# Two attention blocks and an MLP on one core: u's halves moved ahead of three scalings and of the inputs' normalisation, the mask's subtraction moved from VectorE to ScalarE

## The chip, the core and the metric

The kernel runs on one core of one Trainium2 chip. The metric is the device time of one execution in microseconds. Five engines work side by side, each through its own list of instructions in the order in which it was written: TensorE (PE, with its weight loads shown apart as PEld), VectorE (DVE), ScalarE (ACT), GpSimd (POOL), and SyncE (SP), which here issues every DMA. They meet only at semaphores: an instruction waits until a counter has reached a value, and all that is written behind it on its engine waits with it.

## The reference, cut to what matters

For 64 batches of x and ctx, each 128 x 512 in float32:

```python
Mn = Wn @ inorm(x) + bn;  Mm = Wm @ inorm(ctx) + bm        # inorm: normalised over the last axis
A = softmax(Mn.T @ Mm)                                      # 512 x 512
x1 = Wo @ ((Wl @ ctx + bl) @ A.T) + bo + x                  # first attention block
q, k, v = ln(x1) @ q_w + q_b, ctx @ k_w + k_b, ctx @ v_w + v_b     # 16 heads of 32
attn = softmax(where(mask, q @ k.T * scale, lowest))        # mask: one value for each key
hidden = (attn @ v) @ cproj_w + cproj_b + x1                # second attention block
out = hidden + gelu(ln(hidden) @ fc_w + fc_b) @ proj_w + proj_b
```

## The kernel before, in words

Two passes follow each other. `attention_pass` makes `hidden` for all 64 batches, `mlp_pass` makes the output. The change touches the first alone.

Every float32 operand of a large product is split into two halves: `hi`, the value rounded to the format of TensorE's fast float32 (an activation on ScalarE), and `lo`, the rest (a subtraction on VectorE or GpSimd). A product is three matmuls (L966, L967, L968: hi x lo, lo x hi, hi x hi).

The pass is a software pipeline over "slots". In slot s each engine works on several batches at once, each in another stage of its way: b0 = s is in the first block's scores, a1 = s-1 in the transposition of its A, b1 = s-2 in u and the output of the first block (x1), b2 = s-3 in V and the transposition of the normalised x1, b3 and b4 in the second block's scores and softmax, b5 = s-6 in the output projection, and `ahead` = s+1 in the normalisation of its inputs. There are 70 slots; those in the middle are a loop whose body holds four. Even and odd slots differ in one thing: a pair of batches shares the projection to the queries (L688 on ScalarE) in the one kind and to the keys (L682) in the other. Below they are called slots of queries and slots of keys. Nothing but the order in the code sets the order on an engine.

What stands around the change in one slot:

- TensorE: scores of the second block (four matmuls with the mask, L1053, then 64 small ones, L1058), V, the transposition of x1n (L997), Mn and Mm, the first half of queries or keys, the first block's scores, attn @ v (L1099), U = ctxT x at in twelve matmuls, the second half of queries or keys, OUT0 = Wo Wl x u (three matmuls that read `u_hi` and `u_lo`, in the profile `bank<-m_lo,small_hi` and its two neighbours, since u lies in the tile m), and the output projection (reads `qc`).
- ScalarE: exponentials, the hi half of outT (L732), four scalings of A by the reciprocal of its row sums (L738), the hi half of u (L742), the hi halves of the transposed A in four pieces (L710, two and two, with the bias of queries or keys between), the hi halves of the two normalised inputs (L751), the hi half of ctxT (L758).
- VectorE: two transpositions of A's blocks (L842), the lo half of outT (L805), the normalisation of the two inputs of `ahead` (L913), two more transpositions (L842), the lo half of u (L805 again), the transposition of ctx (L926), x1 (L931) and its statistics (L934), the mask less one (L939), hid (L952), maxima of the second scores (L829), x1n, which is x1 normalised (L851).
- GpSimd: at_lo in four pieces (L599), the lo halves of the inputs (L614), the deviation of x1 (L620), x1 plus a bias (L626, tile `stage`), the lo half of ctxT (L629), then the other two pieces of at_lo. VectorE's x1n waits for L626, since it overwrites x1 which L626 reads.
- SyncE: all loads in one queue. The load of the next inputs (L438, L439) waits for the normalisation L913, since it overwrites x_ctx; behind it stand p_blocks, a_turn (A written to DRAM), blocks, hidden, and the next slot's a_blocks (A read back, which waits for a_turn to have landed and for at_lo).

The mask of the second block is loaded as bytes; `mask_less_1` is mask - 1 in bfloat16, and TensorE adds it, times the largest value, to the scores.

Of the kernel before, what the change touches and what calls it, by code (L numbers as in the profile page):

```python
# [18 lines left out]
ALU = mybir.AluOpType  # L19
ACT = mybir.ActivationFunctionType  # L20
AX_X = mybir.AxisListType.X

P = 128
# [164 lines left out]
def attention_pass(nc, x, ctx, mask, w, hidden, mlp):  # L188
# [3 lines left out]
    DC = D // P  # L192
# [4 lines left out]
    with ExitStack() as stack:  # L197
        def sb(name, shape, dt=F32):
            return stack.enter_context(nc.sbuf_tensor(name, shape, dt))
# [68 lines left out]
        rsum0 = sb("rsum0", [P, DC])  # L268
# [3 lines left out]
        x1_rstd = sb("x1_rstd", [P, 1])  # L272
        mask_u8 = sb("mask_u8", [P, 2, P], U8)
        mask_less_1 = sb("mask_less_1", [P, P], BF16)
        negmax1 = sb("negmax1", [P, 4, 4])
        sum1 = sb("sum1", [P, 4, 4])
        rsum1 = sb("rsum1", [P, 4, 4])
# [150 lines left out]
        def _(sp):  # L428
# [78 lines left out]
            def slot(s):  # L507
                if (s + -1).exists():
                    read_a(s + -1)
                e = s + -2  # L510
                if e.exists():
                    if e.has_before(1):
                        after(x1_set, (e + -1).nth(1, 1))
                    else:
                        sp.wait_ge(wow_copied, 2)
                    sp.dma_start(x_res, x[e.number]).then_inc(x_res_loaded, 16)
                e = s + -4
                if e.exists():
                    u = e.parity
                    if e.has_before(2):  # L520
                        after(mask_set, (e + -2).nth(1, 1))
                    else:
                        sp.wait_ge(consts_set, 3)
                    sp.dma_start(mask_u8[0:P:32, u, :],
                                 mask[e.number].partition_broadcast(4)).then_inc(mask_loaded[u], 16)
                if s.first():
                    load_weight(C_W)
                if (s + -5).exists():
                    write_probs(s + -5, 0)
                    write_probs(s + -5, 1)  # L530
                e = s + 2
                if e.exists() and e.has_before(2):
                    load(e)
                if (s + -5).exists():
                    read_probs(s + -5)
                if s.exists():
                    write_a(s, 0)
                    write_a(s, 1)
                e = s
                if e.exists() and e.has_before(1):  # L540
                    load_blocks(e)
                e = s + -6
                if e.exists():
                    after(hid_set, e.nth(1, 1))
                    sp.dma_start(hidden[e.number], hid[:]).then_inc(hid_stored[e.parity], 16)
# [23 lines left out]
        def _(pool):  # L569
# [1 line left out]
            pool.wait_ge(ident_zero, 1)  # L571
            pool.affine_select(out=ident[:], in_=ident[:], compare_op=ALU.not_equal, fill=1.0, base=0,
                               pattern=[[-1, P]], channel_multiplier=1).then_inc(ident_set, 1)
            pool.wait_ge(consts_set, 3)

            def lower_halves(i):

# [67 lines left out]
        def _(act):  # L645
# [18 lines left out]
            def slot(s):  # L664
# [52 lines left out]
                def exp0(t):  # L717
                    if b0.exists():
                        if t == 0 and a1.exists():
                            act.wait_ge(a_written, a1.nth(32, 32))  # L720
                        act.wait_ge(max0_set, b0.nth(4, t + 1))
                        act.activation(A[:, :, t, :], by_chunk(S0_BANK[t]), ACT.Exp,  # L722
                                       bias=negmax0[:, t:t + 1],
                                       accum_out=sum0[:, t:t + 1]).then_inc(exp0_done, 1)

                exp0(0)
                exp0(1)
                exp0(2)
# [5 lines left out]
                    first_weights(1)  # L734
                if b0.exists():
                    act.wait_ge(rsum0_set, b0.nth(1, 1))
                    for t in range(DC):
                        act.activation(A[:, :, t, :], A[:, :, t, :], ACT.Identity,  # L738
                                       scale=rsum0[:, t:t + 1]).then_inc(a_scaled, 1)
                if b1.exists():  # L740
                    act.wait_ge(u_done, b1.nth(1, 1))
                    act.activation(u_hi, bank[U_BANK][:], ACT.Copy).then_inc(u_hi_set, 1)  # L742
                upper_at(0)
                upper_at(1)
                qk_bias(1)
# [2 lines left out]
                if ahead.exists():  # L748
                    for i in range(2):
                        act.wait_ge(normed_set, ahead.nth(2, i + 1))  # L750
                        act.activation(normed_hi[:, i, :], normed[:, i, :], ACT.Copy).then_inc(normed_hi_set, 1)  # L751
                if a1.exists():
                    act.wait_ge(ctxT_turned, a1.nth(1, 1))
                    if b2.exists():
                        act.wait_ge(v_done, b2.nth(1, 1))
                        if s.parity == 1:
                            act.wait_ge(k_done, b2.pair_nth(2, 2))
                    act.activation(pair_half(ctxT_hi, a1), ctx_chunks, ACT.Copy).then_inc(ctxT_hi_set, 1)  # L758
# [4 lines left out]
        def _(dve):  # L763
            dve.memset(masked_bf[:], MASKED).then_inc(consts_set, 1)
            dve.memset(neghalf[:], -0.5).then_inc(consts_set, 1)
            dve.memset(mask_u8[:], 0).then_inc(consts_set, 1)
            dve.wait_ge(consts_set, 3)

            def prepare_small():
                dve.wait_ge(small_in, 16 * 8)  # L770
# [40 lines left out]
            def slot(s):  # L811
# [91 lines left out]
                if b5.exists():  # L903
                    dve.wait_ge(outT_hi_set, b5.nth(1, 1))
                    lower(outT_lo, bank[PV_BANK][:], outT_hi, outT_lo_set)
                if ahead.exists():

                    dve.wait_ge(in_rstd_ready, ahead.nth(1, 1))
                    if b0.exists():
                        dve.wait_ge(m_done, b0.nth(2, 2))  # L910
                        dve.wait_ge(normed_lo_set, b0.nth(2, 2))
                    for i, src in enumerate((x_in, ctx_in)):
                        dve.tensor_scalar(normed[:, i, :], src, in_mv[:, i, 0:1],  # L913
                                          in_rstd[:, i:i + 1], ALU.subtract, ALU.mult).then_inc(normed_set, 1)
                turn_a(2)
                turn_a(3)
                if b1.exists():
                    dve.wait_ge(u_hi_set, b1.nth(1, 1))
                    lower(u_lo, bank[U_BANK][:], u_hi, u_lo_set)
                if b5.exists() and not b4.exists():  # L920
                    first_group()
                if a1.exists():
# [5 lines left out]
                if b1.exists():  # L928
# [3 lines left out]
                                             in1=x_res, op0=ALU.add, op1=ALU.add).then_inc(x1_set, 1)  # L932
                    dve.wait_ge(x1_set, b1.nth(1, 1))
                    dve.bn_stats(x1_stats[:], x1[:]).then_inc(x1_stat, 1)  # L934
                if b3.exists():
                    dve.wait_ge(mask_loaded[b3.parity], b3.dma())
                    if b3.has_before(1):
                        dve.wait_ge(s1_done, (b3 + -1).nth(1, 1))
                    dve.tensor_scalar(mask_less_1[:], mask_u8[:, b3.parity, :], -1.0, None,  # L939
                                      ALU.add).then_inc(mask_set, 1)  # L940
                if b1.exists():
                    dve.wait_ge(x1_stat, b1.nth(1, 1))
                    dve.sem_inc(stats_seen, 1)
# [517 lines left out]
```

## Time and profile before

| | us |
|---|---|
| median of 3 runs | 3034.93 |
| the 3 runs | 3034.93, 3034.04, 3037.51 |
| the profiled execution | 3036.39 |
| its span in the trace | 3034.5 |
| PE busy | 2864.3 (94%) |
| DVE busy | 1910.4 (63%) |
| ACT busy | 1469.5 (48%) |
| POOL busy | 1119.3 (37%) |

The attention pass takes the first 1665 us of the span, roughly; the MLP pass takes the rest and keeps TensorE busy nearly without a gap. Times in a trace are counted from the start of the span. Rows of a timeline give start, duration, engine, line, operation, the written and the read tiles, and how many like instructions were merged; in square brackets stands how long the engine had been idle before it and what ended that. The chain that ended last runs through the MLP pass alone and says nothing of the attention pass.

### The profile page before, as it was taken

The numbers are of one execution on the slowest core, as the hardware profiler recorded it, in microseconds if no ns is written. First come the engines' busy times: TensorE is split into PE (matmuls) and PEld (weight loads), VectorE is DVE, ScalarE is ACT, GpSimd is POOL, SyncE is SP. The second block draws the span as 40 slices with busy tenths as digits, with TensorE's granted clock in tenths as the row PEclk, the third lists the DMA queues.
The fourth block names the chain that finished last, engine by engine and source line by source line (L and its number), as shares of the span: only waits on it lengthen the run. The fifth ranks groups of instructions, "written<-read, shape, count | busy, mean of one in ns | idle before, by whom it ended". The sixth has DMA issues, their size and how long they took to land. (4 is left out here: it accounts for less than half of the span.)

```text
span 3034.5 us, 54536 instructions
## 1 busy us (share of the span) xinstructions
PE 2864.3 (94%) x17527; PEld 2369.3 (78%) x17527; DVE 1910.4 (63%) x3705; ACT 1469.5 (48%) x4210; POOL 1119.3 (37%) x998
## 2 busy tenths in 40 slices
PE   5899999999999999999977999999999999999999
PEld 3777777777777777777765888888888888888887
DVE  5799899999989899999855433333333333333332
ACT  5788778887878877888743211111111111111111
POOL 5566666666666666666632000000000000000000
PEclk7999999999999999999997999999999999999999
DMA  6588888888888888888863210101111111011110
GB/s 184 164 237 230 231 238 229 239 229 235 232 227 237 228 235 236 232 235 232 226 175 129 69 40 17 41 28 41 41 41 41 29 27 39 30 41 41 41 28 14
DMA packets 440889, 416.65 MB, mean 137 GB/s; under 512 B 155200, under 2 KB 319552, under 8 KB 440768
## 3 DMA queue, kind: packets, MB, share of 16 engines
q1 hardware_dynamic: 440768, 415.40, 49.4%
q14 instruction: 89, 0.73, 0.1%
q8 instruction: 32, 0.52, 0.1%
HBM read 231.79 MB, written 167.77 MB: 132 GB/s over the span
## 5 line engine op out<-in xcount | busy, mean ns | idle before, releaser
L1306 ACT ACTIVATE gl<-pre,fc_bias 128x512 f32<-128x512 f32 x256 | 176.6, 690 | 1119.4 <-PE pre L1391 1119.4
L1345 DVE CAST hT_hi<-gl 128x512 fp32r<-128x512 f32 x256 | 109.3, 427 | 840.2 <-ACT gl L1306 840.2
L673 ACT ACTIVATE rows<-bank,negmax 128x128 f32<-128x128 f32 x1024 | 364.2, 394 | 209.2 <-DVE negmax L829 198.9
L599 POOL TENSOR_TENSOR at_lo<-a_blocks,at_hi 128x512 fp32r<-128x512 f32 x256 | 335.4, 1330 | 190.1 <-ACT at_hi L710 190.1
L590 POOL TENSOR_TENSOR rows<-rows,rsum 128x512 f32<-128x512 f32 x256 | 266.0, 1040 | 271.4 <-DVE rsum L825 271.4
L177 POOL TENSOR_TENSOR rstd<-ve,neghalf 128x4 f32<-128x4 f32 x16 | 16.3, 1018 | 870.9 <-DVE ve L171 870.9
L1390 PE MATMUL pre<-yT_hi,rest_lo 128*128 128x512 f32 x768 | 298.9, 389 | 0.0
L1389 PE MATMUL acc<-rest_lo,hT_hi 128*128 128x512 f32 x768 | 298.9, 389 | 0.0
L1391 PE MATMUL acc<-rest_hi,hT_hi 128*128 128x512 f32 x768 | 298.9, 389 | 0.0
L1391 PE MATMUL pre<-yT_hi,rest_hi 128*128 128x512 f32 x768 | 298.8, 389 | 0.0
L1389 PE MATMUL pre<-yT_lo,rest_hi 128*128 128x512 f32 x768 | 298.8, 389 | 0.0
L1390 PE MATMUL acc<-rest_hi,hT_lo 128*128 128x512 f32 x768 | 298.8, 389 | 0.0
L673 ACT ACTIVATION_READ_ACCUMULATOR rows<-bank,negmax 128x1 f32 x1024 | 239.9, 234 | 0.0
L1266 POOL TENSOR_TENSOR rows<-rows,proj_bias 128x512 f32<-128x512 f32 x64 | 82.9, 1298 | 326.4 <-DVE y L183 321.2
L829 DVE TENSOR_REDUCE negmax<-bank 128x4 f32<-128x512 f32 x256 | 169.0, 682 | 36.7 <-PE bank L1058 36.7
L722 ACT ACTIVATE rows<-bank,negmax 128x512 f32<-128x512 f32 x256 | 178.0, 782 | 10.5 <-DVE negmax L835 10.5
L1347 DVE TENSOR_TENSOR hT_lo<-gl,hT_hi 128x512 fp32r<-128x512 f32 x256 | 177.3, 692 | 8.8
L738 ACT ACTIVATE rows<-rows,rsum 128x512 f32<-128x512 f32 x256 | 164.3, 714 | 26.8 <-DVE rsum L900 26.8
L842 DVE STREAM_TRANSPOSE a_blocks<-a_blocks 128x512 f32<-128x512 f32 x256 | 166.2, 687 | 8.3 <-DMA a_blocks<-a_turn 7.6
L614 POOL TENSOR_TENSOR normed_lo<-x_ctx,normed_hi 128x512 fp32r<-128x512 f32 x128 | 162.2, 1289 | 23.5 <-ACT normed_hi L751 23.4
L835 DVE TENSOR_REDUCE negmax<-bank 128x1 f32<-128x512 f32 x256 | 161.4, 667 | 10.2 <-PE bank L968 10.1
L1389 PEld LDWEIGHTS pre<-yT_lo,rest_hi 128*128 128x128 f32 x768 | 144.3, 188 | 30.0
(158 smaller groups left out, 7886.1 us busy)
## 6 DMA issues: line engine op xcount, KB each, us to landing
a_turn<-rows SPq DMA_DIRECT2D x128, 512.0 KB, 7.6
a_blocks<-a_turn SPq DMA_DIRECT2D x256, 256.0 KB, 5.0
p_turn<-rows SPq DMA_DIRECT2D x128, 512.0 KB, 4.5
p_blocks<-p_turn SPq DMA_DIRECT2D x256, 256.0 KB, 5.9
x_ctx<-in_x SPq DMA_DIRECT2D x64, 256.0 KB, 2.6
x_ctx<-in_ctx SPq DMA_DIRECT2D x64, 256.0 KB, 2.9
blocks<-in_ctx SPq DMA_DIRECT2D x256, 64.0 KB, 5.5
small<-in_x SPq DMA_DIRECT2D x64, 256.0 KB, 5.9
```

The costliest lines, as they stand in the source:

```text
L590: pool.tensor_tensor(probs[:, :, r, :, :], probs[:, :, r, :, :], rsum1[:, r, :].unsqueeze(1).unsqueeze(3).to_broadcast([P, 4, 4, 32]), ALU ...
L599: pool.tensor_tensor(by_rows(at_lo, j), a_chunks[:, j], by_rows(at_hi, j).bitcast(F32), ALU.subtract).then_inc(at_lo_set, 1)
L673: act.activation(probs[:, :, r, c, :], by_chunk(S1_BANK[r])[:, c, :].rearrange("p (d b) -> p d b", b=32), ACT.Exp, bias=negmax1[:, r, c:c ...
L722: act.activation(A[:, :, t, :], by_chunk(S0_BANK[t]), ACT.Exp, bias=negmax0[:, t:t + 1], accum_out=sum0[:, t:t + 1]).then_inc(exp0_done, 1)
L738: act.activation(A[:, :, t, :], A[:, :, t, :], ACT.Identity, scale=rsum0[:, t:t + 1]).then_inc(a_scaled, 1)
L829: dve.tensor_reduce(negmax1[:, r, :], by_chunk(S1_BANK[r]), AX_X, ALU.max, negate=True).then_inc(max1_set, 1)
L842: dve.transpose(a_chunks[:, j], a_chunks[:, j]).then_inc(at_turned, 1)
L1306: act.activation(gl[:, i % 2, :], pre[i % 2][:], ACT.Gelu_apprx_tanh, bias=mlp.fc_bias[:, i:i + 1]).then_inc(gelu_done, 1)
L1347: dve.tensor_tensor(hT_lo[:, i % 2, :], gl[:, i % 2, :], hT_hi[:, i % 2, :].bitcast(F32), ALU.subtract).then_inc(hT_lo_set, 1)
L1389: pe.matmul(out, a_hi, b_lo, start=first, stop=False)
L1390: pe.matmul(out, a_lo, b_hi, start=False, stop=False)
L1391: return pe.matmul(out, a_hi, b_hi, start=False, stop=last)
```

## The change: what it does

On ScalarE the hi half of u comes after the first of the four scalings of A instead of after the fourth. On VectorE the lo half of u comes right behind the lo half of outT, ahead of the inputs' normalisation and of two transpositions. The mask less one is made by ScalarE (an activation with a bias tile of -1.0 that VectorE sets once at the start), behind the hi halves of the inputs, and is gone from VectorE. Four constants are set at the start instead of three.

```diff
@@ ScalarE, slot(s)
+                def scale_a(t):
+                    if b0.exists():
+                        act.activation(A[:, :, t, :], A[:, :, t, :], ACT.Identity,
+                                       scale=rsum0[:, t:t + 1]).then_inc(a_scaled, 1)
...
                 if b0.exists():
                     act.wait_ge(rsum0_set, b0.nth(1, 1))
-                    for t in range(DC):
-                        act.activation(A[:, :, t, :], A[:, :, t, :], ACT.Identity,
-                                       scale=rsum0[:, t:t + 1]).then_inc(a_scaled, 1)
+                scale_a(0)
                 if b1.exists():
                     act.wait_ge(u_done, b1.nth(1, 1))
                     act.activation(u_hi, bank[U_BANK][:], ACT.Copy).then_inc(u_hi_set, 1)
+                scale_a(1)
+                scale_a(2)
+                scale_a(3)
                 upper_at(0)
...
+                if b3.exists():
+                    if b3.first():
+                        act.wait_ge(consts_set, 4)
+                    act.wait_ge(mask_loaded[b3.parity], b3.dma())
+                    if b3.has_before(1):
+                        act.wait_ge(s1_done, (b3 + -1).nth(1, 1))
+                    act.activation(mask_less_1[:], mask_u8[:, b3.parity, :], ACT.Identity,
+                                   bias=minus_one[:]).then_inc(mask_set, 1)
@@ VectorE, slot(s)
+                if b1.exists():
+                    dve.wait_ge(u_hi_set, b1.nth(1, 1))
+                    lower(u_lo, bank[U_BANK][:], u_hi, u_lo_set)
                 if ahead.exists():
...
                 turn_a(2)
                 turn_a(3)
-                if b1.exists():
-                    dve.wait_ge(u_hi_set, b1.nth(1, 1))
-                    lower(u_lo, bank[U_BANK][:], u_hi, u_lo_set)
...
-                if b3.exists():
-                    dve.wait_ge(mask_loaded[b3.parity], b3.dma())
-                    if b3.has_before(1):
-                        dve.wait_ge(s1_done, (b3 + -1).nth(1, 1))
-                    dve.tensor_scalar(mask_less_1[:], mask_u8[:, b3.parity, :], -1.0, None,
-                                      ALU.add).then_inc(mask_set, 1)
```

VectorE in one slot of the loop before, from the transpositions of A to hid (m_lo behind a_blocks is first the lo half of outT, then that of u; x_ctx is the normalisation):

```order
L842 STREAM_TRANSPOSE a_blocks<-a_blocks 128x16x32 x2
L805 TENSOR_TENSOR m_lo<-bank,m_hi 128x512
L913 TENSOR_SCALAR x_ctx<-x_ctx,in_mv,in_rstd 128x512 x2
L842 STREAM_TRANSPOSE a_blocks<-a_blocks 128x16x32 x2
L805 TENSOR_TENSOR m_lo<-bank,m_hi 128x512
L926 STREAM_TRANSPOSE small_t<-blocks 128x512
L931 SCALAR_TENSOR_TENSOR x<-bank,out_bias,small 128x512
L934 BN_STATS x_stats<-x 128x6
L939 TENSOR_SCALAR mask_less<-mask_u 128x128
```

And after the change, at the same place:

```order
L858 STREAM_TRANSPOSE a_blocks<-a_blocks 128x16x32 x2
L821 TENSOR_TENSOR m_lo<-bank,m_hi 128x512 x2
L932 TENSOR_SCALAR x_ctx<-x_ctx,in_mv,in_rstd 128x512 x2
L858 STREAM_TRANSPOSE a_blocks<-a_blocks 128x16x32 x2
L942 STREAM_TRANSPOSE small_t<-blocks 128x512
L947 SCALAR_TENSOR_TENSOR x<-bank,out_bias,small 128x512
L950 BN_STATS x_stats<-x 128x6
L954 BN_AGGR x_mv<-x_stats 128x2
```

The two lo halves are now neighbours; the normalisation and the third and fourth transposition stand one instruction later, what follows stands where it was, and the mask is gone.

ScalarE in one slot before, from the hi half of outT to that of ctxT:

```order
L732 ACTIVATE m_hi<-bank 128x512
L738 ACTIVATE rows<-rows,rsum 128x4x128 x4
L742 ACTIVATE m_hi<-bank 128x512
L710 ACTIVATE at_hi<-a_blocks 128x4x4x32
L751 ACTIVATE normed_hi<-x_ctx 128x512
L758 ACTIVATE ctxT_hi<-small_t 128x4x128
```

And after the change:

```order
L738 ACTIVATE m_hi<-bank 128x512
L729 ACTIVATE rows<-rows,rsum 128x4x128
L746 ACTIVATE m_hi<-bank 128x512
L729 ACTIVATE rows<-rows,rsum 128x4x128 x3
L711 ACTIVATE at_hi<-a_blocks 128x4x4x32
L758 ACTIVATE normed_hi<-x_ctx 128x512
L765 ACTIVATE mask_less<-mask_u,minus_one 128x128
L773 ACTIVATE ctxT_hi<-small_t 128x4x128
```

The hi half of u stands behind one scaling, three follow it, and the mask stands between the inputs' hi halves and ctxT's. TensorE's, GpSimd's and SyncE's instructions keep their order.

## Rows read from the trace of the kernel before

**Rows 1.** Busy time by stretch: time, PE, PEld, DVE, ACT, POOL, clock, DMA share, GB/s.
```profile
144.00:1494.00 1350.00, 1276.45 (x10095) 1057.99 (x10094) 1222.51 (x2395) 1080.48 (x3420) 889.91 (x799) 1.00 0.84 233
```

**Rows 2.** Waits, 144 to 1494 us: in total, times, longest.
```profile
PE bank L966 <- DVE m_lo L805: 70.1, 57, 1.8
POOL at_lo L599 <- ACT at_hi L710: 168.9, 57, 3.0
```

**Rows 3.** Timeline of TensorE in one slot of queries.
```profile
1056.41 0.39 PE L968 MATMUL bank<-at_hi,ctxT_hi 128*128 128x512 f32 x1
...
1060.64 0.47 PE L966 MATMUL bank<-m_lo,small_hi 128*128 128x512 f32 x1 [0.97 <-DVE m_lo L805]
...
1064.26 0.40 PE L1053 MATMUL bank<-mask_less,masked_bf 1*128 1x512 bf16 x4
...
1068.44 0.63 PE L997 MATMUL bank<-ident,x 128*128 128x128 f32 x4
```

**Rows 4.** Timeline of ScalarE in the same slot.
```profile
1056.02 2.56 ACT L738 ACTIVATE rows<-rows,rsum 128x512 f32<-128x512 f32 x4 [0.36 <-DVE rsum L900]
1058.49 0.57 ACT L742 ACTIVATE m_hi<-bank 128x512 fp32r<-128x512 f32 x1
1058.97 1.14 ACT L710 ACTIVATE at_hi<-a_blocks 128x512 fp32r<-128x512 f32 x2
...
1061.77 1.15 ACT L751 ACTIVATE normed_hi<-x_ctx 128x512 fp32r<-128x512 f32 x2
...
1066.35 0.37 ACT L673 ACTIVATE rows<-bank,negmax 128x128 f32<-128x128 f32 x1 [2.92 <-DVE negmax L829]
```

**Rows 5.** Timeline of VectorE in the same slot.
```profile
1055.92 1.31 DVE L842 STREAM_TRANSPOSE a_blocks<-a_blocks 128x512 f32<-128x512 f32 x2
1057.15 0.65 DVE L805 TENSOR_TENSOR m_lo<-bank,m_hi 128x512 fp32r<-128x512 f32 x1
1057.72 0.99 DVE L913 TENSOR_SCALAR x_ctx<-x_ctx,in_mv,in_rstd 128x512 f32<-128x512 f32 x2
...
1059.84 0.65 DVE L805 TENSOR_TENSOR m_lo<-bank,m_hi 128x512 fp32r<-128x512 f32 x1
...
1063.10 0.75 DVE L939 TENSOR_SCALAR mask_less<-mask_u 128x128 bf16<-128x128 uint8 x1
...
1065.63 1.29 DVE L829 TENSOR_REDUCE negmax<-bank 128x4 f32<-128x512 f32 x2 [0.57 <-PE bank L1058]
1066.87 1.42 DVE L851 TENSOR_SCALAR x<-x,x_mv,x_rstd 128x512 f32<-128x512 f32 x1
```

**Rows 6.** Timeline of GpSimd in the same slot.
```profile
1059.67 2.52 POOL L599 TENSOR_TENSOR at_lo<-a_blocks,at_hi 128x512 fp32r<-128x512 f32 x2 [2.98 <-ACT at_hi L710]
1062.47 2.54 POOL L614 TENSOR_TENSOR normed_lo<-x_ctx,normed_hi 128x512 fp32r<-128x512 f32 x2 [0.28 <-ACT normed_hi L751]
...
1065.46 1.31 POOL L626 TENSOR_TENSOR stage<-x,cproj_bias 128x512 f32<-128x512 f32 x1
1066.71 1.30 POOL L629 TENSOR_TENSOR ctxT_lo<-small_t,ctxT_hi 128x512 fp32r<-128x512 f32 x1
```

**Rows 7.** Timeline of TensorE in the next slot, one of keys.
```profile
1079.63 0.39 PE L968 MATMUL bank<-at_hi,ctxT_hi 128*128 128x512 f32 x1
...
1084.33 0.47 PE L966 MATMUL bank<-m_lo,small_hi 128*128 128x512 f32 x1 [1.44 <-DVE m_lo L805]
...
1092.04 0.63 PE L997 MATMUL bank<-ident,x 128*128 128x128 f32 x4
```

**Rows 8.** Timeline of ScalarE in that slot of keys.
```profile
1079.61 2.57 ACT L738 ACTIVATE rows<-rows,rsum 128x512 f32<-128x512 f32 x4 [0.36 <-DVE rsum L900]
```

**Rows 9.** Timeline of VectorE, late, while GpSimd is idle.
```profile
1555.77 0.54 DVE L851 TENSOR_SCALAR x<-x,x_mv,x_rstd 128x512 f32<-128x512 f32 x1
```

**Rows 10.** Waits of SyncE's queue, 144 to 1494 us.
```profile
SPq L432 <- DVE x_ctx L913: 159.5, 56, 3.3
SPq L432 <- DMA a_turn<-rows: 27.9, 41, 1.7
```

**Rows 11.** Waits of VectorE, 144 to 1494 us.
```profile
DVE a_blocks L842 <- DMA a_blocks<-a_turn: 1.8, 4, 0.6
```

**Rows 12.** Timeline of TensorE near the end of the attention pass.
```profile
1529.89 0.47 PE L966 MATMUL bank<-m_lo,small_hi 128*128 128x512 f32 x1 [1.66 <-DVE m_lo L805]
```

**Rows 13.** Busy time by stretch, around the one fall of the clock.
```profile
845.50:855.50 10.00, 9.54 (x66) 7.57 (x67) 7.35 (x13) 4.28 (x14) 7.98 (x8) 0.83 0.92 275
```

More of the change, by code:

```diff
@@ L274, in attention_pass @@
         mask_less_1 = sb("mask_less_1", [P, P], BF16)
+        minus_one = sb("minus_one", [P, 1])
         negmax1 = sb("negmax1", [P, 4, 4])
@@ L522, in slot @@
                     else:
-                        sp.wait_ge(consts_set, 3)
+                        sp.wait_ge(consts_set, 4)
                     sp.dma_start(mask_u8[0:P:32, u, :],
@@ L573, in _ @@
                                pattern=[[-1, P]], channel_multiplier=1).then_inc(ident_set, 1)
-            pool.wait_ge(consts_set, 3)
+            pool.wait_ge(consts_set, 4)
             def lower_halves(i):
@@ L765, in _ @@
             dve.memset(neghalf[:], -0.5).then_inc(consts_set, 1)
+            dve.memset(minus_one[:], -1.0).then_inc(consts_set, 1)
             dve.memset(mask_u8[:], 0).then_inc(consts_set, 1)
-            dve.wait_ge(consts_set, 3)
+            dve.wait_ge(consts_set, 4)
             def prepare_small():
```

## The prediction

> **What bounds the kernel now.** I read the busy times by stretch first. From 144 to 1494 us TensorE is busy 1276 of 1350 us at the full clock [rows 1]: 57 slots of the loop's kind, one every 23.6 us. The waits of that stretch name one thing for which TensorE stands still: the lo half of u, 70.1 us in 57 times, 1.23 us a slot [rows 2]. That is what the change attacks. The question is what is late next, and for that I took the timelines of one slot, engine by engine.
>
> The slot of queries that I follow ends with TensorE's transposition of x1n at 1068.44 [rows 3], the slot of keys behind it with the one at 1092.04 [rows 7]: 23.60 us. In the first TensorE ends U at 1056.80, does the second half of the queries, and waits 0.97 us for u_lo before 1060.64 [rows 3]. ScalarE makes u_hi only at 1058.49, behind four scalings that began at 1056.02 [rows 4]; VectorE makes u_lo at 1059.84, behind the normalisation and two transpositions [rows 5]. So both moves hit the cause of the wait.
>
> But another chain ends at the same transposition. at_hi on ScalarE starts at 1058.97 [rows 4]; its first piece releases GpSimd, which had waited 2.98 us (and waits so in all 57 slots, 168.9 us [rows 2]); GpSimd then works at_lo, normed_lo (0.28 us of waiting for normed_hi), the deviation and `stage` without a pause until 1066.77 [rows 6]. VectorE's x1n starts 0.10 us later, 1066.87, and ends at 1068.29 [rows 5]; TensorE's transposition starts at 1068.44 [rows 3], 0.15 us after it, which is also the distance of u_lo's end (1060.49) from its reader (1060.64). The maxima ahead of x1n end their issue at 1066.83 or so (the second of the pair 0.60 after the first, x1n one more 0.60 on): VectorE was free 0.04 us before x1n was released. So two chains arrive within 0.05 us of each other: TensorE's own through u_lo, and ScalarE's and GpSimd's through x1n. The transposition then releases xnT_hi on ScalarE, which from there to at_hi waits on nothing but the row sums. The second chain is a ring that closes once a slot, and its length is the period.
>
> **The change part by part.**
>
> *u_hi behind one scaling.* One scaling takes 0.617 us of issue: (1058.49 - 1056.02) / 4 [rows 4]. In the slot of queries u_hi could start at 1056.64, but U ends at 1056.80, and a release from TensorE takes ScalarE about 0.04: start at 1056.84. It was 1058.49, so 1.65 us earlier. The price is 0.20 us of idle ScalarE, since the three scalings and at_hi now stand behind a wait that was never felt: at_hi(0) starts at 1056.84 + 0.48 + 3 x 0.617 = 1059.17, not 1058.97. In a slot of keys U ends at 1080.02 [rows 7] and the first scaling at 1079.61 + 0.617 = 1080.23 [rows 8]: no wait and at_hi where it was. Bounds for the wait in queries: 0 if U's modelled end is 0.2 late, 0.35 if the release costs as much as TensorE's 0.15; I take 0.19.
>
> *u_lo ahead of the normalisation.* VectorE ends the issue of outT_lo at 1057.72 [rows 5]; u_hi is there at 1057.41. u_lo then runs 1057.72 to 1058.37, 2.1 us earlier, and TensorE, ready at 1060.64 - 0.97 = 1059.67 at the earliest, finds it done. In keys it is ready at 1082.89 [rows 7] and finds it done too. The wait of 1.23 us goes wholly. The normalisation and the next two transpositions move back by 0.58 us (1057.72 - 1057.15). Their readers on ScalarE stand at 1060.73 or later: transposition 3 ends at 1059.8, 4 at 1060.4, the normalisation at 1059.3 against 1061.96. Covered by 0.5 us or more. SyncE's load of the next inputs, released by it, and p_blocks and a_turn behind it move back by 0.58 us; that is rival 1.
>
> *The mask.* VectorE loses 0.75 us [rows 5] in a stretch where it waits for TensorE anyway (0.57 us ahead of the maxima). Worth nothing by itself. On ScalarE no row has an activation from bytes; the nearest by size is the 128x128 exponential, 0.37 us [rows 4], the largest of the tail 0.62 for 128x512. I take 0.37. It starts when normed_hi's issue ends, 1061.77 + 0.19 + 1.04 = 1063.00, and is set at about 1063.45. TensorE, no longer held by u_lo, would start the scores at 1064.26 - 0.97 = 1063.3: it waits 0.15 to 0.25 us there, and about 0.4 in keys. ctxT_hi behind it slips by 0.5 us; its reader starts at 1066.71 [rows 6], covered by 3 us.
>
> ScalarE's rules in the Trainium skill ("ScalarE: Activation LUTs", Rules for kernel authors) say to keep an add on VectorE, not ScalarE. This case's rows do not bear it out for this tile: 0.75 us on VectorE here, beside 0.37 for the like size on ScalarE.
>
> *What is late next.* From the scores to the transposition TensorE needs 4.18 us (1064.26 to 1068.44) [rows 3], so it would be there at 1063.45 + 4.18 = 1067.63. x1n cannot be: its chain starts with at_hi(0), 0.19 us later than before, so it ends at 1068.48 and the transposition starts at 1068.63. TensorE waits 1.0 us there. In keys it waits the same while x1n comes as before. The wait for u_lo turns into one for x1n; the period of queries becomes 23.77, that of keys stays 23.6.
>
> The sum against the profiled execution, 3036.4:
> - 29 of the 57 slots are of queries: 29 x 0.19 = +5.5 us.
> - Where a_blocks lands late, VectorE's wait (1.8 us in 4 times [rows 11], and 0.3 once for nothing shown) reached TensorE through u_lo; now u_lo has 1 us of room: -1.8.
> - Near the end, where nothing is loaded ahead, 1.66 us are lost to u_lo once [rows 12]; it moves two transpositions (1.2 us) forward: -1.2.
> - Around 850 us the clock's mean over 10 us is 0.83 [rows 13], so 1.7 of the 10 us were lost, right after a wait for u_lo. The longest of these waits (1.8 us [rows 2]) go, shorter ones come: I count half and a little for its neighbours, -1.0.
> - The queue's delay, a few slots: +1.0.
> Together +2.5: 3038.9 for such an execution. The median of the runs lies 1.5 below the profiled one, so 3037.5.
>
> **The rivals.**
>
> 1. *Slower: the load queue becomes the ring.* SyncE already waits for a_turn's landing before it may read a_blocks in 41 of 57 slots, 0.68 us each [rows 10], and a_blocks then reaches VectorE late in 4 [rows 11]. The normalisation releases the load 56 times [rows 10]; 0.58 us later there means a_turn lands later, a_blocks too, the transpositions too, and with them the next normalisation: each slip is handed on. It costs something from the point where the slip of the transpositions is over about 0.5 us (then ScalarE's third and fourth at_hi are late). Against it: DMA is at 0.84 [rows 1], and 53 of 57 slots show no wait. If a third of the slots lose a further 0.4 us: 19 x 0.4 = 7.6, 3045.
> The Trainium skill ("SBUF — State Buffer", Who interferes with whom) makes it sharper: a tensor_scalar of VectorE in a two-port mode and a GpSimd instruction hold that pair in turn, whole instructions long, and the loser stands still. The trace agrees: x1n takes 1.42 us beside L629 [rows 5, 6] and 0.54 with GpSimd idle [rows 9]. The normalisation now ends 0.3 us before at_lo starts at 1059.67; a slip of 1 us would put it behind a piece of at_lo, 1.2 us.
>
> 2. *Faster: the x1n ring is not what I take it for.* Then the mask bounds: set at 1063.45, transposition 1067.63, a period of 22.8, and by the same working 22.5 in keys: 57 x 0.95 = -54, 2981. Against it: x1n follows `stage` by 0.10 us in the row, and nothing moved feeds that chain earlier.
>
> 3. *Same, a little faster: U's end costs ScalarE nothing* (the lower bound above). The +5.5 goes: 3032.
>
> 4. *Slower: the clock.* TensorE's one wait becomes two, before the scores and before the transposition. If that halves the clock for a few us now and then as at 850, each time costs 1.7 us [rows 13]; three to four times decide: 3044.
>
> 5. *The change does nothing to the wait*: u_lo is still late. VectorE's order rules it out.
>
> **How the numbers follow.** Less than 0.2% (6 us) cannot be told from no change. The forecast has 0.55, with a range of its own of 3033 to 3042; rival 1 has 0.19, rival 2 0.04, rival 3 0.15, rival 4 0.06, rival 5 0.01. Slower than 3041.0: rivals 1 and 4 and 0.04 of the forecast's upper tail, 0.29. Faster than 3028.9: rival 2 and 0.03 of rival 3, 0.07. Same: 0.64. The range that holds 8 in 10: 3031 to 3045.
>
> **What would show it.** Right: no wait for u_lo in the stretch, waits of about 1 us of the transposition L997 for x1n and of 0.1 to 0.4 of the scores for the mask; x1n still 0.10 us behind `stage`; ScalarE idle 0.2 us before u_hi in every other slot; periods 23.8 and 23.6 in turn. Wrong: a period under 23 us (rival 2), transpositions of A waiting for a_blocks in many slots (rival 1), a clock under 1.00 in the loop (rival 4).

## The result, and the profile after

The changed kernel takes 3044.5 us in the median of 8 runs (3037.1 to 3055.5), the kernel before 3034.9 (3031.5 to 3037.5). The ratio is 1.0031, with a 95% interval of 1.002 to 1.0042: slower by 0.3%, and its runs lie three times as far apart. The execution in the trace took 3040.9 us, one of the shorter ones.

The wait that the change attacks is all but gone from TensorE's waits between 144 and 1494 us; two others stand where there was one (us in total, times, longest):

```profile
PE bank L1007 <- DVE x L867: 46.1, 55, 0.9
PE bank L1063 <- ACT mask_less L765: 31.9, 56, 2.4
PE bank L976 <- DVE m_lo L821: 0.8, 2, 0.6
```

Before, the last of these alone was there, with 70.1 us in 57 times [rows 2]. Now 46.1 + 31.9 + 0.8 = 78.8.

One slot of queries of the changed kernel, TensorE first. U ends at 1060.88, OUT0 follows with no wait for u_lo, the scores wait for the mask, the transposition waits for x1n:

```profile
1060.49 0.39 PE L978 MATMUL bank<-at_hi,ctxT_hi 128*128 128x512 f32 x1
...
1063.59 0.40 PE L976 MATMUL bank<-m_lo,small_hi 128*128 128x512 f32 x1
...
1067.63 0.40 PE L1063 MATMUL bank<-mask_less,masked_bf 1*128 1x512 bf16 x4 [0.45 <-ACT mask_less L765]
...
1072.69 0.63 PE L1007 MATMUL bank<-ident,x 128*128 128x128 f32 x4 [0.81 <-DVE x L867]
```

ScalarE in the same slot. The first scaling takes 0.617 us of issue in [rows 4], and u_hi now starts 0.81 us after it: 0.19 us of waiting for U. at_hi starts 3.14 us after the first scaling, before 2.95:

```profile
1060.11 0.73 ACT L729 ACTIVATE rows<-rows,rsum 128x512 f32<-128x512 f32 x1 [0.35 <-DVE rsum L916]
1060.92 0.60 ACT L746 ACTIVATE m_hi<-bank 128x512 fp32r<-128x512 f32 x1
1061.41 1.94 ACT L729 ACTIVATE rows<-rows,rsum 128x512 f32<-128x512 f32 x3
1063.25 1.14 ACT L711 ACTIVATE at_hi<-a_blocks 128x512 fp32r<-128x512 f32 x2
...
1067.09 0.40 ACT L765 ACTIVATE mask_less<-mask_u,minus_one 128x128 bf16<-128x128 uint8 x1
```

VectorE: the two lo halves side by side, the normalisation at 0.98 us for two as before, and an idle 0.86 us ahead of x1n, which starts 0.11 us after GpSimd's `stage` has ended (1071.02):

```profile
1061.23 1.25 DVE L821 TENSOR_TENSOR m_lo<-bank,m_hi 128x512 fp32r<-128x512 f32 x2
1062.40 0.98 DVE L932 TENSOR_SCALAR x_ctx<-x_ctx,in_mv,in_rstd 128x512 f32<-128x512 f32 x2
...
1071.13 1.42 DVE L867 TENSOR_SCALAR x<-x,x_mv,x_rstd 128x512 f32<-128x512 f32 x1 [0.86 <-POOL stage L627]
```

```profile
1069.73 1.29 POOL L627 TENSOR_TENSOR stage<-x,cproj_bias 128x512 f32<-128x512 f32 x1
```

The distance from one transposition to the next is 23.75 us in slots of queries and 23.58 in slots of keys (medians); before it was 23.59 and 23.61. That is the first cost. The second is in three slots of this trace, 25.6, 26.2 and 24.8 us long. In the longest, VectorE waits for a_blocks, and the normalisation then takes 2.94 us for two instead of 0.98:

```profile
798.55 1.30 DVE L858 STREAM_TRANSPOSE a_blocks<-a_blocks 128x512 f32<-128x512 f32 x2 [1.34 <-DMA a_blocks<-a_turn]
799.77 1.25 DVE L821 TENSOR_TENSOR m_lo<-bank,m_hi 128x512 fp32r<-128x512 f32 x2
800.95 2.94 DVE L932 TENSOR_SCALAR x_ctx<-x_ctx,in_mv,in_rstd 128x512 f32<-128x512 f32 x2
```

GpSimd had begun its two pieces of at_lo 0.07 us earlier. Shown one by one, each of the two instructions of the normalisation takes 1.5 us, where one alone takes 0.53:

```profile
800.88 1.28 POOL L600 TENSOR_TENSOR at_lo<-a_blocks,at_hi 128x512 fp32r<-128x512 f32 x1 [2.98 <-ACT at_hi L711]
```

```profile
800.95 1.50 DVE L932 TENSOR_SCALAR x_ctx<-x_ctx,in_mv,in_rstd 128x512 f32<-128x512 f32 x1
802.37 1.51 DVE L932 TENSOR_SCALAR x_ctx<-x_ctx,in_mv,in_rstd 128x512 f32<-128x512 f32 x1
```

The first ends 0.29 us after GpSimd's first piece (802.16), the second 0.28 us after its second (803.60). ScalarE then stands 2.50 us before its third at_hi, and GpSimd 2.76 us before normed_lo, so the whole ring is later:

```profile
800.88 2.72 POOL L600 TENSOR_TENSOR at_lo<-a_blocks,at_hi 128x512 fp32r<-128x512 f32 x2 [2.98 <-ACT at_hi L711]
806.36 2.50 POOL L615 TENSOR_TENSOR normed_lo<-x_ctx,normed_hi 128x512 fp32r<-128x512 f32 x2 [2.76 <-ACT normed_hi L758]
```

```profile
804.54 1.22 ACT L711 ACTIVATE at_hi<-a_blocks 128x512 fp32r<-128x512 f32 x2 [2.50 <-DVE a_blocks L858]
```

The first of the three long slots, 382.0 to 407.6 us, has a second cause in it. TensorE stands for 1.52 us before the scores, and its granted clock then falls to the lower of its two levels, 1.2 GHz, until about 406.6: a matmul of V takes 0.63 us instead of 0.40, and the mean clock of ten us is 0.83, as around the fall of before [rows 13]. The transposition follows V without a pause, though x1n had ended at 406.81:

```profile
401.93 0.40 PE L1063 MATMUL bank<-mask_less,masked_bf 1*128 1x512 bf16 x4 [1.52 <-ACT mask_less L765]
...
404.47 0.63 PE L976 MATMUL bank<-first_lo,ctxT_hi 128*128 128x512 f32 x1
...
407.60 0.60 PE L1007 MATMUL bank<-ident,x 128*128 128x128 f32 x4
```

```profile
405.40 1.41 DVE L867 TENSOR_SCALAR x<-x,x_mv,x_rstd 128x512 f32<-128x512 f32 x1 [0.83 <-POOL stage L627]
```

```profile
400.00:410.00 10.00, 8.48 (x65) 6.74 (x64) 7.81 (x13) 5.46 (x16) 8.16 (x7) 0.83 1.00 278
```

With the 0.15 us from x1n to its reader, the clock costs 407.60 - 406.96 = some 0.6 us of this slot (an estimate).

The waits of VectorE and of SyncE's queue, 144 to 1494 us, show how near to being late a_blocks is in other slots. a_blocks is late 26 times instead of 4 [rows 11], and SyncE waits for a_turn's landing 54 times instead of 41 [rows 10]:

```profile
DVE a_blocks L858 <- DMA a_blocks<-a_turn: 12.5, 26, 1.3
```

```profile
SPq L433 <- DMA a_turn<-rows: 66.5, 54, 2.4
```

The long slots (over 24.1 us) and the slow normalisations are the same ones. In the traces of the changed kernel, of u_only, of two_scalings and of norm_later, the last three described below, an instruction of the normalisation took 1.4 us or more in exactly the 3, 4, 10 and 48 long slots, and at most 0.55 us in all the others.

### The profile page after: what moved, and what is told of

It reads as the page before. It is cut to its first block and busy times, and to the rows that moved or that the text cites. A ratio compares the mean times of both kernels' runs of the same rounds, so it can differ in the third digit from the quotient of the medians.

```text
span 3039.0 us, 54525 instructions
## 1 busy us (share of the span) xinstructions
PE 2858.2 (94%) x17527; PEld 2367.8 (78%) x17527; DVE 1880.2 (62%) x3642; ACT 1493.0 (49%) x4274; POOL 1119.6 (37%) x998
## 5 line engine op out<-in xcount | busy, mean ns | idle before, releaser
L729 ACT ACTIVATE rows<-rows,rsum 128x512 f32<-128x512 f32 x256 | 170.4, 715 | 26.0 <-DVE rsum L916 26.0
```

The costliest lines, as they stand in the source:

```text
L729: act.activation(A[:, :, t, :], A[:, :, t, :], ACT.Identity, scale=rsum0[:, t:t + 1]).then_inc(a_scaled, 1)
```

## The experiments

Three statements were to be told apart: that the first part of the loss is the ring through x1n (0.17 us in every second slot) and the gain is missing because that ring was as long as TensorE's own; that the rest of the loss is late a_blocks pushing the normalisation beside at_lo; and, against both, that the mask's move costs.

For all kernels: the median time and the ratio to the kernel before with its interval; from one trace each, the median distance between transpositions in slots of keys and of queries, how many of 56 slots are over 24.1 us, and VectorE's waits for a_blocks (times, us).

| kernel | us | ratio | keys, queries | long | a_blocks |
|---|---|---|---|---|---|
| before | 3034.9 | | 23.61, 23.59 | 4 | 4, 1.8 |
| changed | 3044.5 | 1.0031 [1.0020, 1.0042] | 23.58, 23.75 | 3 | 26, 12.5 |
| u_only | 3047.8 | 1.0043 [1.0030, 1.0056] | 23.62, 23.76 | 4 | 25, 16.4 |
| mask_only | 3034.1 | 0.9995 [0.9986, 1.0004] | 23.61, 23.59 | 0 | 1, 0.3 |
| two_scalings | 3050.1 | 1.0049 [1.0034, 1.0063] | 23.59, 23.58 | 10 | 34, 22.9 |
| norm_first | 3039.6 | 1.0014 [1.0005, 1.0022] | 23.59, 23.75 | 3 | none |
| both | 3038.7 | 1.0011 [1.0002, 1.0019] | 23.59, 23.56 | 7 | none |
| norm_later | 3134.0 | 1.0330 [1.0316, 1.0343] | 25.66, 25.84 | 48 | 48, 45.9 |
| a_first | 3034.7 | 0.9998 [0.9989, 1.0007] | 23.58, 23.75 | 1 | 1, 0.2 |
| pool_first | 3028.8 | 0.9976 [0.9965, 0.9988] | 23.37, 23.39 | 4 | 50, 47.6 |
| pool_on_before | 3123.5 | 1.0294 [1.0280, 1.0307] | 24.65, 24.62 | 56 | 53, 53.2 |
| pool_split | 2990.7 | 0.9858 [0.9843, 0.9873] | 22.67, 22.54 | 8 | 9, 7.0 |
| pool_split_a_first | 2969.4 | 0.9788 [0.9774, 0.9801] | 22.58, 22.55 | 0 | 10, 5.9 |
| split_on_before | 3027.6 | 0.9972 [0.9962, 0.9982] | 23.53, 23.48 | 1 | 5, 1.5 |

**One part of the change alone.** u_only is the changed kernel with the mask's instruction back on VectorE:

```diff
                 # ScalarE, with its waits
-                    act.activation(mask_less_1[:], mask_u8[:, b3.parity, :], ACT.Identity,
-                                   bias=minus_one[:]).then_inc(mask_set, 1)
                 ...
                 # VectorE, behind the statistics of x1, with its waits
+                    dve.tensor_scalar(mask_less_1[:], mask_u8[:, b3.parity, :], -1.0, None,
+                                      ALU.add).then_inc(mask_set, 1)
```

> The changed kernel with the mask less one back on VectorE, where it stood before; only u's halves are moved. Theory (two costs: the ring ScalarE-GpSimd-x1n is 0.19 us longer in slots of queries, and now and then a late a_blocks pushes the inputs' normalisation into a piece of at_lo on GpSimd, which costs 1 to 3 us each time): the mask has no part in either, so as the changed kernel, 3040 to 3047, ratio to before 1.001 to 1.004, x1n still ends the slots, periods 23.75 and 23.57. Rival (the mask on ScalarE is what costs): back to 3035 or under, ratio 1.000 or less.

Measured 3047.8 (3046.5 to 3050.8), just over the upper end; periods, late a_blocks and long slots as in the changed kernel. The mask has no part in the loss. mask_only is the other half: u's halves where they were, the mask on ScalarE.

> The kernel before with only the mask less one moved to ScalarE, behind the inputs' hi halves; u's halves stay where they were. Theory: VectorE waits for TensorE there anyway and ScalarE's mask is ready about 1 us before TensorE wants it, so nothing moves: 3035, ratio 0.999 to 1.001, the wait for u_lo still 1.2 us a slot. Rival (the mask's move costs): over 1.002. Rival (it gains by itself): under 0.999.

Measured 3034.1, no change, as expected; the wait for u_lo is still there, 66.7 us in 57 times. So the loss belongs to u's halves, within the noise of these runs.

**ScalarE's wait taken away.** two_scalings:

```diff
                 scale_a(0)
+                scale_a(1)
                 if b1.exists():
                     act.wait_ge(u_done, b1.nth(1, 1))
                     act.activation(u_hi, bank[U_BANK][:], ACT.Copy).then_inc(u_hi_set, 1)
-                scale_a(1)
                 scale_a(2)
```

> The changed kernel with u's hi half behind the second scaling instead of the first. ScalarE then no longer waits for U: at_hi starts 14.12 us after the transposition in both kinds of slot, and the period of queries goes from 23.75 back to 23.57 (29 x 0.19 = 5.5 us less). u_hi ends 0.4 us later, so VectorE starts u_lo about 0.2 us later and the normalisation with it: if late a_blocks and the lock of the port are the other cost, slots of 24.8 us and more come oftener than in the changed kernel (3 in the traced run), and eat part of the 5.5. Expected 3037 to 3045. Rival (the whole loss is ScalarE's wait): 3034 to 3036 with no long slots.

The period of queries went to 23.58 as expected: the 0.17 us are ScalarE's wait for U. But the time rose to 3050.1 (3034.9 to 3059.2), outside the expected range: u_hi is there later, VectorE's u_lo and with it the normalisation too, and ten slots are long instead of three. The normalisation starts 13.89 us after the transposition in the median of the loop, in the changed kernel 13.63. The shortest of its runs, 3034.9, would fit a run without long slots, but it has no trace; the others show that the second cost is the larger one.

**The normalisation earlier and later.** norm_first puts it ahead of both lo halves, norm_later behind the third transposition:

```diff
 # norm_first
                 turn_a(0)
                 turn_a(1)
+                <the normalisation of the two inputs>
                 <the lo half of outT>
                 <the lo half of u>
-                <the normalisation of the two inputs>
                 turn_a(2)
 # norm_later
-                <the normalisation of the two inputs>
                 turn_a(2)
+                <the normalisation of the two inputs>
                 turn_a(3)
```

> The changed kernel with VectorE's order turned: two transpositions, the inputs' normalisation, then the lo halves of outT and of u, then two transpositions. The load of the next inputs is released 1.1 us earlier than in the changed kernel. u_lo ends at about 14.0 us after the transposition, before TensorE wants it (14.3 and 14.6). Theory: the long slots go (late a_blocks waits a few or none), the ring's 0.19 us in queries stays: 3036 to 3039 with a narrow spread, ratio 1.000 to 1.0015. Rival (the long slots have another cause, such as the clock): they stay, 3042 and over.

> The changed kernel with the inputs' normalisation one more transposition later on VectorE, 0.6 us: the suspected cost doubled. ScalarE's part is as in the changed kernel. Theory: a_blocks comes late in most slots, and a slip of only 0.3 us already puts the normalisation beside GpSimd's at_lo, so many slots of 24.8 us and more: 3060 to 3090. Rival (the load's delay does not matter): 3040 to 3047 as the changed kernel.

norm_first: no wait for a_blocks at all, 3039.6 between 3037.2 and 3042.9, just over the expected 3039; the ring's 23.75 stays. norm_later: 0.6 us more, and 48 of 56 slots are long, 3134, beyond the 3090 I gave. The cost does not grow evenly with the delay. A slot is either nearly untouched, or the normalisation meets at_lo and the slot is 0.7 to 2.8 us longer than 23.6 (one of the 48, the last, 4.4). Part of it is the clock: its mean in norm_later's loop is 0.98, where the changed kernel has 1.00, and 2% of 1350 us is 27 us, which is the most that it can have cost there (an estimate).

```profile
144.00:1494.00 1350.00, 1218.83 (x9432) 1011.67 (x9431) 1179.18 (x2187) 1036.63 (x3262) 842.54 (x747) 0.98 0.79 218
```

The kernel called both is norm_first with two scalings.

> norm_first with u_hi behind the second scaling: both costs of the change taken away. u_lo would still end by 14.1 us after the transposition, since VectorE now makes the normalisation and outT_lo ahead of it. Theory: 5.5 us less than norm_first (3039.6), so 3033 to 3036, ratio 0.999 to 1.001, no slot over 24.1 us beside what before had; TensorE still waits 1 us a slot for x1n. The whole gain of the 1.2 us wait stays away, since the ring through x1n sets 23.57.

Measured 3038.7, where 3033 to 3036 was expected. The periods are right (23.59, 23.56), but seven slots are long for another reason. Each of them opens with ScalarE idle for 4.9 to 6.0 us before its first exponential. In three of them the trace explains this by nothing ("issue"); in the other four it names VectorE's maxima, of which the first pair had been ready for some three us at 264 us, the one of the four that was looked at. Such pauses come a multiple of some 94 us apart, which is one turn of the loop of four slots; not every one makes its slot long. One of them:

```profile
454.88 0.37 ACT L674 ACTIVATE rows<-bank,negmax 128x128 f32<-128x128 f32 x1 [5.09 <-issue]
```

Counting those that end with "issue", the kernel before has this twice in its loop, the changed kernel not once, norm_first ten times and both eight. What holds ScalarE there was not tested.

**The queue alone.** a_first is the changed kernel with one swap on SyncE; VectorE, ScalarE and GpSimd keep the changed order. write_a writes A to a_turn, read_probs reads p_blocks:

```diff
+                if s.exists():
+                    write_a(s, 0)
+                    write_a(s, 1)
                 if (s + -5).exists():
                     read_probs(s + -5)
-                if s.exists():
-                    write_a(s, 0)
-                    write_a(s, 1)
```

> The changed kernel with one swap in SyncE's queue: A is written to a_turn ahead of the four reads of p_blocks instead of behind them (2 us earlier; p_blocks has some 4 us to spare). VectorE, ScalarE and GpSimd are as in the changed kernel. Theory (long slots come from a late a_blocks): a_blocks waits fall from 26 to a few, no slot over 24.8 us, the ring's 23.75 and 23.57 stay: 3036 to 3040 with a narrow spread. Rival (the moved normalisation costs by itself, whatever the queue): 3042 and over, long slots stay.

3034.7 (3031.8 to 3036.2), 9.9 us less than the changed kernel and even a little under the expected range, with a_blocks late once. The ring's 23.75 and 23.58 stay, and no slot is over 24.14. Some 3 us of the 9.9 lie outside the loop: the swap also shortens the second and third slot (24.87 and 24.37 to 23.65 and 23.75) and one near the end (20.87 to 19.87). The rest fits the long slots: the loop itself is 5.1 us shorter in the two traces, and some 7 us are left of the 9.9 between the medians. SyncE's waits for a_turn's landing, 54 in the changed kernel, are gone altogether. This settles the second cost.

**The ring through x1n cut.** Two orders on GpSimd, each put on the kernel called both and on the kernel before; the second of them with the swap of a_first too, on the kernel called both also without it:

```diff
 # pool_first: deviation of x1 and stage ahead of both lower halves of the inputs
 # pool_split: between them
+                lower_normed(0)
                 if b1.exists():
                     <deviation of x1, then stage>
+                lower_normed(1)
-                <both lower halves, ahead of the deviation>
```

> The kernel called both, with GpSimd's deviation of x1 and its sum x1 plus bias (stage) put ahead of the inputs' two lo halves. The ring through x1n is cut: stage ends about 2 us earlier. Theory: the period falls to what the mask on ScalarE and TensorE allow, 22.5 to 22.9 us, so 57 x 0.8 = 45 us less: 2985 to 2995. Rival (DMA, 0.84 busy, is next and a_blocks comes late in every slot): 3005 to 3030. Rival (the lock of the port delays x1n until GpSimd ends the second lo half): period 23.1, 3008.

> The kernel before with only GpSimd's two instructions moved, u's halves and the mask as they were. Theory (two rings of the same length): TensorE waits for u_lo as before and the period stays at 23.55 or so: 3031 to 3036, ratio 0.999 to 1.001. Rival (only GpSimd's chain ever bounded the kernel): as pool_first, under 3000.

Both missed. pool_first gave 3028.8, near the upper end of its first rival: a_blocks late in 50 of 57 slots. The reason is in GpSimd's waits of the two kernels, pool_first and pool_on_before:

```profile
POOL x_rstd L616 <- DVE x_ve L956: 100.4, 57, 2.4
```

```profile
POOL x_rstd L615 <- DVE x_ve L946: 141.1, 53, 2.8
POOL stage L621 <- DVE hid L952: 71.1, 53, 2.5
```

Moved to the front, the deviation waits 1.8 us a slot for x1's variance, in pool_on_before 2.7 and `stage` 1.3 more for hid, and the last pieces of at_lo, for which the read of a_blocks waits, end 4.5 us after the transposition instead of 2.2. pool_on_before loses 88 us, by this and by the clock, whose mean in its loop is 0.98, and so says nothing of the rings. The order had to fill that wait, and pool_split does; pool_split_a_first adds the swap of a_first.

> The kernel called both with GpSimd's order: first lower half of the inputs, deviation of x1, stage, second lower half (pool_first had both halves behind stage, and GpSimd then waited 1.8 us a slot for x1's variance, which made at_lo and a_blocks late). Theory: stage ends 1.2 us earlier, GpSimd waits little, at_lo ends where it did. The ring through x1n is 22.6 to 22.8 long; the queue's own ring then bounds at about 23.2, with a_blocks late in many slots: 3010 to 3025. Rival (x1n's lock eats the gain): 3033.

> pool_split with A written ahead of the reads of p_blocks. Theory: the queue's ring is 1 to 2 us shorter, so the period falls to what TensorE, the mask and x1n allow, 22.7 to 22.9: 2990 to 3000. Rival (DMA as a whole is full at 0.84 to 0.87): as pool_split, 3010 to 3025.

2990.7 and 2969.4, both some 20 us better than the lower ends of what was expected: a_blocks is late in 9 and 10 slots and not in many, and the period falls to 22.67 and 22.54 in the one, 22.58 and 22.55 in the other, 1.03 us a slot. The gain of pool_split over the kernel called both, 48 us, is that of GpSimd's order alone. In pool_split_a_first `stage` stands between the two lower halves without a wait:

```profile
1040.26 1.29 POOL L615 TENSOR_TENSOR normed_lo<-x_ctx,normed_hi 128x512 fp32r<-128x512 f32 x1 [0.25 <-ACT normed_hi L761]
1041.51 0.55 POOL L623 TENSOR_TENSOR x_rstd<-x_ve,neghalf 128x1 f32<-128x1 f32 x1
1042.03 1.28 POOL L629 TENSOR_TENSOR stage<-x,cproj_bias 128x512 f32<-128x512 f32 x1
1043.27 1.29 POOL L615 TENSOR_TENSOR normed_lo<-x_ctx,normed_hi 128x512 fp32r<-128x512 f32 x1
```

and TensorE is busy 1324.6 of the 1350 us, where it was 1276.5 [rows 1]:

```profile
144.00:1494.00 1350.00, 1324.64 (x10586) 1110.74 (x10586) 1217.14 (x2424) 1138.51 (x3632) 921.08 (x827) 1.00 0.90 243
```

The last run puts the same two edits on the kernel before.

> The kernel before, u's halves and the mask where they were, with the two edits that took pool_split_a_first to 2969: GpSimd's deviation of x1 and stage between the two lower halves of the inputs, and A written ahead of the reads of p_blocks. Theory (two rings of one length, one through u_lo, one through x1n): cutting only the second leaves the first, so the period stays 23.5 to 23.6 and TensorE still waits 1.2 us a slot for u_lo: 3031 to 3036, ratio 0.998 to 1.000. Rival (GpSimd's chain alone bounded the kernel and the change under study gave nothing even then): 2970 to 2990.

3027.6, a little under the expected 3031, periods 23.53 and 23.48, and TensorE's wait for u_lo to the tenth what it was [rows 2]:

```profile
PE bank L969 <- DVE m_lo L808: 70.1, 57, 1.7
```

So the two edits without u's move give 7 us, u's move (and the mask's) without them loses 10 (4 with the normalisation first and two scalings, the kernel called both), and all together give 65. That fits two rings of one length, neither of which is worth much while the other stands. How much of the 7 is GpSimd's order and how much the swap in the queue was not told apart: neither was run alone on the kernel before in this form.

## Why the prediction was right or wrong

The forecast was 3037.5, within 0.2% of before; measured were 3044.5 and +0.31%. The time lies inside the range of 8 in 10, at its upper end, and outside the forecast's own range of 3033 to 3042. What came is the ring of the forecast with rival 1 on top of it, which had 0.19 and was given 3045; that the range held it is due to this rival and not to the sum.

- *What bounds the kernel*: right. The step that two chains arrive within 0.05 us of each other, and that the one through x1n is late next, holds: x1n starts 0.11 us after `stage`, TensorE waits for it in 55 of 57 slots, the period falls by 1 us only when GpSimd's order is changed too (pool_split), and by 0.1 us when it is changed without u's move (split_on_before).
- *u_hi behind one scaling*: right. 0.19 us of wait in queries, none in keys; a period of 23.75 against the 23.77 forecast. two_scalings takes it away. The term +5.5 is (23.75 - 23.59) x 29 = 4.6.
- *u_lo ahead of the normalisation*: the wait went, as said, but for 0.8 us in two slots. "Covered by 0.5 us or more" held in an undisturbed slot and failed where a_blocks was late.
- *The mask*: right, no cost and no gain in mask_only. 0.40 us in the trace for the 0.37 taken. TensorE's wait for it was 0.45 in the slot of queries, not 0.15 to 0.25; it lies within the room that x1n leaves and costs nothing.
- *What is late next*: TensorE waits 0.81 us for x1n, said 1.0.
- *The sum*: the term of the queue was mis-sized. It was put at +1.0 for a few slots. In the traced execution the three long slots alone are 1.9 + 2.7 + 1.2 = 5.8 over their neighbours, of which the clock has some 0.6, and in the median of the runs the queue costs some 7 us in the loop (a_first). The working was there: the load 0.58 us later, SyncE waiting for a_turn in 41 slots. The prediction let the 53 slots without a wait for a_blocks count against it, though they only said that the slip before was under the room left, not how much room there was. And it priced a meeting with at_lo at 1.2 us, one piece. The slot lost 1.2 in the mildest case, where one of the two instructions of the normalisation stood behind one piece, and 2.7 where each stood behind a piece of its own, and then ScalarE and GpSimd behind them.
- The late a_blocks of before (-1.8) and the half price of the clock (-1.0) were taken off as if nothing took their place. The clock fell in the changed kernel's loop once, as it did before (0.83 over ten us in both), now behind the 1.52 us wait for the mask: nothing shows the -1.0, and of rival 4 no more than this one fall came. The late a_blocks rose instead of going. The last slots gained 1.1 us (63.6 to 62.5 from the loop's end to the last transposition), said 1.2. The stretch ahead of the loop was 1.1 us longer, 0.9 of it ahead of the first transposition, which was not counted.
- The chance of 0.29 for slower named the right cause. One result cannot show that it was too low, but a mechanism that hands its slip on from slot to slot, with under 0.5 us of room, looks worth more than 0.19.

Where the normalisation began 0.07 us behind at_lo's first piece, its two instructions ended 0.29 us after the first piece and 0.28 us after the second, 1.50 and 1.51 us long instead of 0.53. The Trainium skill ("SBUF — State Buffer", Who interferes with whom) says that, of VectorE in a two-port mode and GpSimd, the one that issues first has their shared pair of ports for its whole instruction and the other is blocked meanwhile. The trace agrees: each of the two waited for one instruction of GpSimd.

One correction to the text ahead of the prediction: the slots run from -1 to 69, so there are 71, not 70. No number of the prediction uses it.

## What to carry to other kernels

When a wait is to be removed from the busiest engine, follow the other chains into the point where its slot closes, and subtract: here the second one was 0.05 us behind the first, so that taking away 70 us of waiting was worth nothing until that chain was shortened too, and 48 us when it was (from the kernel called both to pool_split). An instruction that is moved back by half a microsecond takes with it the DMA that it releases and everything behind that in the queue; look for the wait at the far end of that queue, and count how often it is already near zero room. A step that alone makes a kernel slower can be part of one that makes it 2.1% faster.

## What the runs showed of the hardware that I had not expected

- The normalisation of VectorE beside a GpSimd instruction is not slowed in proportion: 0.98 us for two when GpSimd is idle, 2.94 when GpSimd began a pair of pieces 0.07 us earlier, each of the two ending 0.3 us after a piece. In a timeline this is no wait with a releaser but a longer instruction. In norm_later, 0.6 us of delay cost 89 us over the changed kernel by this, by the late a_blocks behind it, and in part by the clock (0.98 in the mean).
- ScalarE's pauses at its first exponential, one turn of the loop or a multiple of it apart, that end with "issue": 2 times before (5.1 us), 10, 8, 4 and 5 times (3.2 to 5.8 us) in norm_first, both, pool_first and pool_split, in which the inputs' load is issued earlier, and once in pool_on_before, in which it is not; never in the changed kernel, nor in pool_split_a_first. Pauses as long are also put down to VectorE's maxima. Their cause stays open.
- One swap of two DMA groups in a queue, with the same bytes, was worth 21 us between pool_split and pool_split_a_first; DMA's share of busy time rose from 0.86 to 0.90. Most of it is not waiting for a_blocks (7.0 and 5.9 us): the trace of pool_split has eight long slots, together 15 us over 22.6 each, which all open with such a pause of ScalarE of 4.8 to 5.6 us, and pool_split_a_first has none.
